# VectorE adds the residual rows before it divides the probabilities, in the steps that hold both

## The chip, the core and the metric

The kernel runs on one core of a Trainium2 chip. TensorE (PE) multiplies matrices into the accumulators (PSUM), VectorE (DVE), ScalarE (ACT) and GpSimd (POOL) do the elementwise work, SyncE (SP) issues the transfers. Each works through its own queue in order and waits for the others on counters (semaphores). The metric is the device time of one execution in microseconds; lower is better.

## What is computed

A decoder layer on x of 16 samples, 256 rows and 512 columns: windowed attention with 32 query heads and 8 key heads and a sink in each softmax, a convolution mixer on a second input, and a linear map by the mean of eight factors. Each is added to x behind a layer norm. The change lies in the attention:

```python
logits = jnp.einsum('bqhmd,bkhd->bhmqk', q, k) * SM_SCALE
...
e = jnp.exp(logits - m)
exp_sink = jnp.exp(s - m)
w = e / (jnp.sum(e, axis=-1, keepdims=True) + exp_sink)
out = jnp.einsum('bhmqk,bkhd->bqhmd', w, v).reshape(Bv, Tv, N_HEADS * HEAD_DIM)
return out @ out_w.T + out_b
...
x = x + _L0_attn_ref(_layernorm(x, axis=-1), ...)
```

## The kernel before

The attention goes over the 16 samples twice: the first sweep with one half of the heads, the second with the other (their weights are loaded and split between the two). A **window** is one sample in one sweep; there are 32. The first sweep writes x plus its half of the output projection to memory, the second adds its half to that and makes the layer norm for the mixer.

All engines run the same schedule, written out by hand. A loop body holds two windows, that is p = 0 to 7 and j = 0, 1; each (p, j) is a **step**, and a window has eight, numbered 2 * (p % 4) + j = 0 to 7. The bodies 2 to 6 and 10 to 14 are loops on the chip, the others are written out. The stages of a window are spread over three: while the projections ("units") of one window run, the scores of it and the output projection of the one before last are made.

TensorE does in a step: transposes of the divided probabilities (line 539, `pP`), a unit (lines 507, 514, `wP`) in steps 0, 1, 3, 5, 6 and 7, transposes of normalised rows in steps 2 and 4 (lines 462, 472), the scores (line 529, `sP`) in even steps, the value product (line 553, `vP`), and parts of the output projection (line 574, `oP`): 1, 2, 1, 2 and 1 of them in steps 1 to 5, and one in step 7. `oP` is a single accumulator. Parts 0 to 3 make tile t = 0 of the rows (128 of 256), begun in step 7 and ended in step 2; parts 4 to 7 make tile t = 1, steps 3 to 5. The first part of a tile waits until VectorE has added the tile before (`x1_ready`).

VectorE does in a step: `divide` (lines 856, 858, 864: the sum `den` of exponentials and sink, its reciprocal, four multiplications of `pr`) for the scores of the step before, `mask_transposed` (line 873, `pT`), in steps 3 and 7 `residual` (line 895: `x1` = `oP` + `xb`), then the rotation `turned` of a unit (line 823, `m1`) or the values (line 831), `mask_min` (lines 841, 847: mask the scores, take the row's minimum), `o_low` (line 882), and parts of layer norms (lines 778 to 790). `residual` of tile 0 stands in step 3, that of tile 1 in step 7.

ScalarE copies the transposed tile (line 655), adds the bias to a unit (line 633, `m2`), and takes the exponentials of the step's scores (lines 646, 649, `es`). GpSimd multiplies `m2` by its table (line 717), adds the two products (line 726), shifts the sinks (line 734), and in the first sweep, in step 2, adds the output bias to `xb` (line 759), two instructions for the two tiles; `residual` waits for both (`xb_ready`), in the second sweep for the transfer of `xb` instead.

The functions `residual_tile`, `divide`, `mask_transposed`, `residual` and VectorE's `body` are those that the change touches or moves.

Of the kernel before, what the change touches and what calls it, by code (L numbers as in the profile page):

```python
# [85 lines left out]
def attention_part(nc, x, wqkv, bqk, bv, wout, bout, sinks, rope, masks, ident, factors, ssm_pad, dcoef,  # L86
# [3 lines left out]
    with ExitStack() as ctx:  # L90
# [130 lines left out]
        def wait(eng, s, value):  # L221

            if isinstance(value, int) and value <= 0:
                return
            eng.wait_ge(s, value)
# [44 lines left out]
        def late(y, lag, p):  # L270

            if y.number is None:
                return y.sweep == 1
            return 2 * y.number + p // 4 - lag >= B
# [8 lines left out]
        def unit_of(p, j):  # L283
            return UNIT_AT.get(2 * (p % 4) + j)
# [8 lines left out]
        def residual_tile(y, p, j):  # L293

            return None if y.first else RESIDUAL_AT.get(2 * (p % 4) + j)
# [479 lines left out]
        def _(dve):  # L775
# [76 lines left out]
            def divide(y, u, j):  # L852
                h = 16 * y.m + 2 * u + j
                s = (2 * u + j) % 4
                dve.wait_ge(es_ready, h + 1)
                dve.tensor_tensor(den[:, s], ac[:, s], es[:, s], ALU.add).then_inc(den_ready, 1)  # L856
                dve.wait_ge(den_ready, h + 1)
                dve.reciprocal(rden[:, s], den[:, s]).then_inc(rden_ready, 1)
                dve.wait_ge(rden_ready, h + 1)
                for a in range(2):  # L860
                    for t in range(NT):
                        cols = slice(t * P, (t + 1) * P)
                        i = 2 * a + t
                        last = dve.tensor_scalar(pr[:, s, a, cols], pr[:, s, a, cols], rden[:, s, i:i + 1], None, ALU.mult)  # L864
                last.then_inc(pn_ready, 1)
# [19 lines left out]
            def residual(y, p, t):  # L885

                r = y.window(p) - 2
                old = late(y, 2, p)
                if old:
                    dve.wait_ge(xb_landed, 16 * r + 16)  # L890
                else:
                    dve.wait_ge(xb_ready, r + 1)
                dve.wait_ge(out_done, 8 * r + 4 * t + 4)
                wait(dve, x1_stored, 16 * r)
                dve.tensor_tensor(x1[:, t, :], oP[:], xb[:, t, :], ALU.add).then_inc(x1_ready, 1)  # L895
# [23 lines left out]
            def body(y):  # L919
                for p in range(8):  # L920
                    for j in range(2):
                        u, jj = (p - 3, 1) if j == 0 else (p - 2, 0)
                        if y.here(u, 0):
                            divide(y, u, jj)
                        if y.here(p, 3):
                            mask_transposed(y, p, j)
                        if residual_tile(y, p, j) is not None:
                            residual(y, p, residual_tile(y, p, j))
                        n = unit_of(p, j)
                        if n is not None and not y.drain:  # L930
                            if y.first and n == V_UNIT and p < 4:
                                dve.wait_ge(c_in, 16 * NCONST)
                            if n == V_UNIT:
                                v_evac(y, p)
                            else:
                                turned(y, p, rope_index(n))
                        if x_next(y, p, j):
                            x_low(y.window(p) + 1, (p // 4 + 1) % 2, p % 4 - 1)
                        if y.here(p, 2):
                            mask_min(y, p, j)  # L940
                        u, jj = (p - 4, 1) if j == 0 else (p - 3, 0)
                        if y.here(u, 0):
                            o_low(y, u, jj)
                        sl = 2 * (p % 4) + j
                        if sl in (4, 6) and x_after(y, p):
                            ln1_stats(y.window(p) + 2, (sl - 4) // 2)
                        if y.first and p == 0:
                            for t in range(NT):
                                if j == 0:
                                    ln1_stats(1, t)  # L950
                                else:
                                    ln1_end(1, t)
                        elif sl in (0, 1) and fresh(y, p):
                            ln1_end(y.window(p) + 1, sl)
                        if sl == 4 and late(y, 2, p):
                            ln2_stats(y.window(p) - 2, 0)
                        if sl == 0 and late(y, 3, p):
                            ln2_stats(y.window(p) - 3, 1)
                        if sl in (1, 2) and late(y, 3, p):
                            ln2_end(y.window(p) - 3, sl - 1)  # L960
                        for i, n in split_now(y, p, j):
                            split_low(i, n)
# [460 lines left out]
```

## Time and profile before

| | us |
|---|---|
| runs of the kernel | 2184.93, 2185.22, 2189.57 |
| their median | 2185.22 |
| the profiled execution | 2187.89 |
| its span, first to last instruction | 2185.7 |
| TensorE busy in it | 1988.6 |
| VectorE busy | 1610.8 |
| ScalarE busy | 935.4 |
| GpSimd busy | 771.3 |

The attention takes the stretch to about 1685 us, the rest is the mixer and the linear map, which the change doesn't touch. Times of the trace are counted from the span's start. An idle time in brackets stands behind the instruction that it precedes, with the work that ended it. In a row of merged instructions "x4" is their number, and the time is from the start of the first to the end of the last; instructions of one engine overlap a little, so that the next starts before the one ahead has ended. "issue" is time in which the engine waited for nothing that the profile shows.

### The profile page before, as it was taken

The page shows a single profiled execution, that of the slowest core. Times are in us where ns is not written, and L with a number is a line of the kernel's source. Part 1 is how long each engine was busy: PE and PEld are TensorE (multiplying, and loading weights), DVE is VectorE, ACT ScalarE, POOL GpSimd, SP SyncE. Part 2 cuts the span into 40 slices and gives each one's busy share as a digit, 9 for nine tenths or more (in the row PEclk, how much of TensorE's full clock was granted, in tenths as well). Part 3 has the DMA queues.
Part 4 walks back from the last instruction along what each step waited for, and adds up shares of the span by engine and source line. Part 5 has one row for each costly group of instructions (what it writes and reads, how often), then busy time and mean ns, then how long its engine had stood idle before and what let it go on. Part 6 is the DMA issues. An engine that isn't in the chain of part 4 may idle for free. (4 is left out here: it accounts for less than half of the span.)

```text
span 2185.7 us, 49034 instructions
## 1 busy us (share of the span) xinstructions
PE 1988.6 (91%) x15488; PEld 1619.9 (74%) x15488; DVE 1610.8 (74%) x5784; ACT 935.4 (43%) x3481; POOL 771.3 (35%) x879
## 2 busy tenths in 40 slices
PE   5799999999999989899999999999996899999699
PEld 4688877787877867778778777878774677677587
DVE  4777777776777766667767676767774699999787
ACT  3454545454545444444544454544542222222233
POOL 2244334333333333323322232223330454454354
PEclk8999999999999999999999999999998899999799
DMA  5147111111111121211111111111112633333364
GB/s 184 51 102 150 51 59 48 49 61 56 49 50 49 66 85 56 72 36 68 49 50 49 50 50 56 53 51 49 50 50 66 225 90 86 85 88 88 105 226 157
DMA packets 73966, 170.37 MB, mean 78 GB/s; under 512 B 6928, under 2 KB 15632, under 8 KB 73632
## 3 DMA queue, kind: packets, MB, share of 16 engines
q1 hardware_dynamic: 64160, 146.80, 20.4%
q0 software_dynamic: 3840, 8.39, 2.1%
q10 hardware_dynamic: 5760, 12.59, 1.5%
q8 instruction: 111, 1.82, 0.4%
q14 instruction: 95, 0.78, 0.1%
HBM read 109.03 MB, written 50.41 MB: 73 GB/s over the span
## 5 line engine op out<-in xcount | busy, mean ns | idle before, releaser
L646 ACT ACTIVATE pr<-pr,mx 128x128 f32<-128x128 f32 x1024 | 399.0, 391 | 441.5 <-DVE mx L847 441.5
L717 POOL TENSOR_TENSOR m<-m,rope_sb 128x512 f32<-128x512 f32 x160 | 206.6, 1291 | 563.2 <-ACT m L633 563.2
L514 PE MATMUL wP<-xTh,wh 128*128 128x256 f32 x1280 | 380.5, 297 | 5.8 <-DVE xTl L807 3.5
L514 PE MATMUL wP<-xTl,wh 128*128 128x256 f32 x1280 | 366.1, 286 | 0.0
L514 PE MATMUL wP<-xTh,wl 128*128 128x256 f32 x1280 | 364.7, 285 | 0.0
L1095 PE MATMUL y<-kv,tap 128*128 128x288 f32 x1280 | 330.1, 414 | 27.4 <-DVE res L1143 9.3
L1095 PEld LDWEIGHTS y<-kv,tap 128*128 128x128 f32 x1280 | 240.5, 192 | 116.9 <-issue 24.3
L856 DVE TENSOR_TENSOR den<-ac,es 128x4 f32<-128x4 f32 x256 | 63.1, 246 | 302.0 <-ACT es L649 270.5
L574 PE MATMUL oP<-woh,oTh 128*128 128x512 f32 x512 | 223.3, 436 | 55.0 <-DVE x L895 55.0
L514 PEld LDWEIGHTS wP<-xTh,wh 128*128 128x128 f32 x1280 | 248.7, 194 | 8.5 <-issue 3.1
L514 PEld LDWEIGHTS wP<-xTl,wh 128*128 128x128 f32 x1280 | 248.6, 194 | 0.0
L514 PEld LDWEIGHTS wP<-xTh,wl 128*128 128x128 f32 x1280 | 248.1, 194 | 0.0
L847 DVE CUSTOM_DVE_ANT_0 pr<-sP,mask_sb 128x128 f32<-128x128 f32 x1024 | 235.1, 284 | 0.5
L864 DVE TENSOR_SCALAR pr<-pr,rden 128x128 f32<-128x128 f32 x1024 | 224.6, 283 | 9.1
L553 PE MATMUL vP<-pT,vv 128*64 128x256 f32 (+1 forms) x2048 | 224.5, 340 | 0.9 <-DVE oTl L882 0.9
L633 ACT ACTIVATE m<-wP,bqk_sb 128x256 f32<-128x256 f32 x320 | 134.3, 471 | 210.7 <-PE wP L514 210.5
L734 POOL TENSOR_TENSOR sk<-mx,sink_sb 128x4 f32<-128x4 f32 x256 | 57.4, 224 | 458.8 <-DVE mx L847 458.8
L823 DVE SCALAR_TENSOR_TENSOR m<-wP,bqk_sb,rope_sb 128x256 f32<-128x256 f32 x320 | 139.4, 477 | 105.4 <-ACT m L633 105.0
L529 PE MATMUL sP<-kT,qT 32*128 32x128 f32 (+1 forms) x4096 | 209.7, 342 | 6.7 <-DVE mx L847 6.7
L1045 POOL TENSOR_TENSOR kv<-kk 128x1024 f32<-128x1024 f32 x64 | 144.1, 2251 | 182.8 <-PE y L1095 154.1
L574 PE MATMUL oP<-woh,oTl 128*128 128x512 f32 x512 | 203.8, 398 | 0.0
L574 PE MATMUL oP<-wol,oTh 128*128 128x512 f32 x512 | 203.7, 398 | 0.0
(108 smaller groups left out, 3781.8 us busy)
## 6 DMA issues: line engine op xcount, KB each, us to landing
tap<-padded_taps SPq DMA_DIRECT2D x64, 256.0 KB, 3.4
kk<-in_ctxt SPq DMA_DIRECT2D x64, 192.0 KB, 3.1
x_in<-in_x SPq DMA_DIRECT2D x16, 512.0 KB, 3.7
xt_split<-xTh SPq DMA_DIRECT2D x16, 512.0 KB, 3.1
xt_split<-xTl SPq DMA_DIRECT2D x16, 512.0 KB, 4.2
xb<-in_x SPq DMA_DIRECT2D x16, 512.0 KB, 4.5
fsum<-in_factors POOLq DMA_DIRECT2D x8, 1024.0 KB, 8.6
x_part_rows<-x SPq DMA_DIRECT2D x16, 512.0 KB, 3.1
```

The lines of the kernel that those rows point to most:

```text
L514: last = pe.matmul(wP[:, h * T:(h + 1) * T], w[:, n, c, h * P:(h + 1) * P], a[:, s, c, :], start=(c == 0 and i == 0), stop=(c == KD - 1 an ...
L529: last = pe.matmul(sP[:, r, t * P:P + 2 * t * P], qT[rr, p % 2, h, t * P:(t + 1) * P], kT[rr, kslot, h, 0:(t + 1) * P], start=(h == 0), st ...
L553: last = pe.matmul(vP[a * HD:(a + 1) * HD, k * P:T], vv[:, (u // 4) % 2, k, g * HD:(g + 1) * HD], pT[:, s, a, 2 * k * P:2 * P + k * P], st ...
L574: last = pe.matmul(oP[:], a[:, o, c, t * P:(t + 1) * P], w[:, c, :], start=(c == 0 and n == 0), stop=(c == NO - 1 and n == 2))
L633: last = act.activation(m2[:, s, 1 - half], wP[:, half * T:(half + 1) * T], ACT.Identity, bias=bqk_sb[:, y.sweep, i, half:half + 1])
L646: act.activation(pr[:, s, a, cols], pr[:, s, a, cols], ACT.Exp, bias=mx[:, s, i:i + 1], scale=-1.0, accum_out=ac[:, s, i:i + 1])
L717: pool.tensor_tensor(m2[:, s], m2[:, s], rope_sb[:, 1 if i == 0 else 0, 1:3], ALU.mult).then_inc(sin_ready, 1)
L823: last = dve.scalar_tensor_tensor(m1[:, s, half], wP[:, half * T:(half + 1) * T], bias[:, half:half + 1], tab[:, 0], ALU.add, ALU.mult)
L847: last = dve.tensor_tensor_reduce(pr[:, s, a, t * P:(t + 1) * P], sP[:, 2 * j + a, 2 * t * P:(2 * t + 1) * P], mask_sb[:, t * P:(t + 1) * ...
L864: last = dve.tensor_scalar(pr[:, s, a, cols], pr[:, s, a, cols], rden[:, s, i:i + 1], None, ALU.mult)
L1045: pool.tensor_tensor(kv[:, s, :, 0:4 * n].rearrange("p c (d n) -> p c d n", d=4), k0.unsqueeze(2).broadcast_to([P, KD, 4, n]), shifted, AL ...
L1095: last = pe.matmul(y[:, s, c, 0:NY], tap[:, s, d * P:(d + 1) * P], kv[:, s, c - d, :], start=(d == 0), stop=(d == c))
```

## The change

`residual` moves from behind `mask_transposed` to the front of VectorE's step. It happens in steps 3 and 7 of each window, 64 times in all. In 61 of them a division stands in the same step; at the very end of the attention three have none. The instructions, their waits and all other engines' programs are the same.

```diff
             def body(y):
                 for p in range(8):
                     for j in range(2):
+                        if residual_tile(y, p, j) is not None:
+                            residual(y, p, residual_tile(y, p, j))
                         u, jj = (p - 3, 1) if j == 0 else (p - 2, 0)
                         if y.here(u, 0):
                             divide(y, u, jj)
                         if y.here(p, 3):
                             mask_transposed(y, p, j)
-                        if residual_tile(y, p, j) is not None:
-                            residual(y, p, residual_tile(y, p, j))
```

VectorE in step 3 of the body 1, before; the first row is the last work of step 2, the last one the rotation of step 3:

```order
252 L882 TENSOR_TENSOR oTl<-vP,oTh 128x256
253 L856 TENSOR_TENSOR den<-ac,es 128x4
254 L858 RECIPROCAL rden<-den 128x4
255 L864 TENSOR_SCALAR pr<-pr,rden 128x128 x4
256 L873 TENSOR_TENSOR pT<-pP,mask_sb 128x2x256
257 L895 TENSOR_TENSOR x<-oP,xb 128x512
258 L823 SCALAR_TENSOR_TENSOR m<-wP,bqk_sb,rope_sb 128x256 x2
```

The same place now:

```order
252 L882 TENSOR_TENSOR oTl<-vP,oTh 128x256
253 L895 TENSOR_TENSOR x<-oP,xb 128x512
254 L856 TENSOR_TENSOR den<-ac,es 128x4
255 L858 RECIPROCAL rden<-den 128x4
256 L864 TENSOR_SCALAR pr<-pr,rden 128x128 x4
257 L873 TENSOR_TENSOR pT<-pP,mask_sb 128x2x256
258 L823 SCALAR_TENSOR_TENSOR m<-wP,bqk_sb,rope_sb 128x256 x2
```

The add of line 895 has passed seven instructions (den, the reciprocal, four multiplications and the masked transpose) and stands behind the work of step 2.

VectorE in step 7 of the same body, before; the first two rows are the layer norm at the end of step 6:

```order
316 L784 BN_AGGR mv<-stats 128x2 x2
317 L787 TENSOR_SCALAR veps<-mv 128x2
318 L856 TENSOR_TENSOR den<-ac,es 128x4
319 L858 RECIPROCAL rden<-den 128x4
320 L864 TENSOR_SCALAR pr<-pr,rden 128x128 x4
321 L873 TENSOR_TENSOR pT<-pP,mask_sb 128x2x256
322 L895 TENSOR_TENSOR x<-oP,xb 128x512
323 L823 SCALAR_TENSOR_TENSOR m<-wP,bqk_sb,rope_sb 128x256 x2
```

and now:

```order
316 L784 BN_AGGR mv<-stats 128x2 x2
317 L787 TENSOR_SCALAR veps<-mv 128x2
318 L895 TENSOR_TENSOR x<-oP,xb 128x512
319 L856 TENSOR_TENSOR den<-ac,es 128x4
320 L858 RECIPROCAL rden<-den 128x4
321 L864 TENSOR_SCALAR pr<-pr,rden 128x128 x4
322 L873 TENSOR_TENSOR pT<-pP,mask_sb 128x2x256
323 L823 SCALAR_TENSOR_TENSOR m<-wP,bqk_sb,rope_sb 128x256 x2
```

Here it has passed the same seven and stands behind the layer norm. The rotation follows line 873 directly in both steps.

## Rows read from the trace of the kernel before

**Rows 1.** The page, busy time of each engine, share of the span, instructions.
```profile
PE 1988.6 (91%) x15488; PEld 1619.9 (74%) x15488; DVE 1610.8 (74%) x5784; ACT 935.4 (43%) x3481; POOL 771.3 (35%) x879
```
**Rows 2.** TensorE's waits, 125:780, 780:960, 960:1640: us in total, times, longest.
```profile
PE oP L574 <- DVE x L895: 25.5, 26, 1.2
...
PE oP L574 <- DVE x L895: 14.4, 5, 4.8
...
PE oP L574 <- DVE x L895: 11.7, 14, 1.1
```
**Rows 3.** VectorE in order of time, step 3, first sweep: start, us, instruction.
```profile
430.91 0.98 DVE L856 TENSOR_TENSOR den<-ac,es 128x4 f32<-128x4 f32 x1 [1.48 <-ACT es L649]
...
432.14 0.87 DVE L864 TENSOR_SCALAR pr<-pr,rden 128x128 f32<-128x128 f32 x4
432.93 0.68 DVE L873 TENSOR_TENSOR pT<-pP,mask_sb 128x512 f32<-128x512 f32 x1
433.53 0.68 DVE L895 TENSOR_TENSOR x<-oP,xb 128x512 f32<-128x512 f32 x1
434.13 0.86 DVE L823 SCALAR_TENSOR_TENSOR m<-wP,bqk_sb,rope_sb 128x256 f32<-128x256 f32 x2
...
435.87 0.28 DVE L847 CUSTOM_DVE_ANT_0 pr<-sP,mask_sb 128x128 f32<-128x128 f32 x1
```
**Rows 4.** TensorE in order of time, the same step and the next.
```profile
434.26 0.50 PE L574 MATMUL oP<-woh,oTh 128*128 128x512 f32 x1 [1.09 <-DVE x L895]
...
436.74 1.59 PE L529 MATMUL sP<-kT,qT 32*128 32x128 f32 x32
```
**Rows 5.** GpSimd in order of time, the same step.
```profile
429.33 2.54 POOL L759 TENSOR_TENSOR xb<-xb,bo_sb 128x512 f32<-128x512 f32 x2
433.33 1.27 POOL L717 TENSOR_TENSOR m<-m,rope_sb 128x512 f32<-128x512 f32 x1 [1.46 <-ACT m L633]
```
**Rows 6.** VectorE and TensorE in order of time, step 7, first sweep.
```profile
455.83 0.16 DVE L856 TENSOR_TENSOR den<-ac,es 128x4 f32<-128x4 f32 x1 [0.27 <-ACT es L649]
...
458.36 0.50 PE L574 MATMUL oP<-woh,oTh 128*128 128x512 f32 x1 [0.80 <-DVE x L895]
```
**Rows 7.** VectorE in order of time, steps 5 and 0, first sweep.
```profile
446.44 0.88 DVE L823 SCALAR_TENSOR_TENSOR m<-wP,bqk_sb,rope_sb 128x256 f32<-128x256 f32 x2 [1.12 <-ACT m L633]
...
464.50 0.88 DVE L823 SCALAR_TENSOR_TENSOR m<-wP,bqk_sb,rope_sb 128x256 f32<-128x256 f32 x2 [0.54 <-ACT m L633]
```
**Rows 8.** GpSimd and VectorE in order of time, first body, 70 to 74 us.
```profile
70.83 1.27 POOL L717 TENSOR_TENSOR m<-m,rope_sb 128x512 f32<-128x512 f32 x1 [3.54 <-ACT m L633]
...
71.18 1.59 DVE L864 TENSOR_SCALAR pr<-pr,rden 128x128 f32<-128x128 f32 x4
```
**Rows 9.** GpSimd, VectorE and TensorE in order of time, 780:830.
```profile
784.15 1.31 POOL L717 TENSOR_TENSOR m<-m,rope_sb 128x512 f32<-128x512 f32 x1 [1.02 <-ACT m L633]
...
784.26 1.22 DVE L856 TENSOR_TENSOR den<-ac,es 128x4 f32<-128x4 f32 x1
...
787.85 0.55 PE L574 MATMUL oP<-woh,oTh 128*128 128x512 f32 x1 [4.24 <-DVE x L895]
...
801.15 0.88 DVE L823 SCALAR_TENSOR_TENSOR m<-wP,bqk_sb,rope_sb 128x256 f32<-128x256 f32 x2 [0.76 <-ACT m L633]
...
824.99 0.87 DVE L823 SCALAR_TENSOR_TENSOR m<-wP,bqk_sb,rope_sb 128x256 f32<-128x256 f32 x2 [1.15 <-ACT m L633]
```
**Rows 10.** Second sweep: order of time at steps 3 and 7, VectorE's waits of 960:1640.
```profile
1097.75 0.39 PE L574 MATMUL oP<-wol,oTh 128*128 128x512 f32 x1
...
1102.46 0.88 DVE L823 SCALAR_TENSOR_TENSOR m<-wP,bqk_sb,rope_sb 128x256 f32<-128x256 f32 x2 [2.16 <-ACT m L633]
...
1123.69 0.16 DVE L856 TENSOR_TENSOR den<-ac,es 128x4 f32<-128x4 f32 x1 [1.48 <-ACT es L649]
...
DVE m L823 <- ACT m L633: 59.1, 40, 2.9
```
**Rows 11.** One stretch: each engine's busy us, granted clock, DMA share, GB/s.
```profile
614.10:617.50 3.40, 3.40 (x19) 3.40 (x18) 1.81 (x7) 0.37 (x1) 0.00 (x0) 0.50 0.01 2
```

## The prediction, made before the changed kernel ran

> **What bounds the kernel now.** I read the shares of the page first, then TensorE's waits by stretch, then the order of time around single places of the residual add. TensorE is busy 1988.6 of 2185.7 us, VectorE 1610.8 [rows 1]: TensorE leads, and every stop of it is worth a look. The add (line 895) is waited for by the output projection (line 574) 25.5 us at 26 places in 125 to 780 us, 14.4 us at 5 in 780 to 960, 11.7 us at 14 in 960 to 1640 [rows 2]. These 51.6 us are the most the change could give. TensorE waits in the step in which the add stands: it has done its transposes, its unit and the value product, and needs the output accumulator empty.
>
> But TensorE is not alone on the path. VectorE masks the scores (lines 841, 847), ScalarE takes their exponentials, VectorE divides by their sum, multiplies the transposed tile with its mask (line 873) and only then reaches the next masking. TensorE's next scores wait for that masking. So a stop of TensorE that goes counts only until the next place at which VectorE is late. I go through one window (eight steps, numbered 0 to 7; adds in 3 and 7) for the first half of the heads, and one for the second.
>
> **Step 7, first half (13 places).** The projection waits 0.80 us [rows 6]; of the 25.5 us at 26 places the 13 of step 3 hold 14.5 (1.00 to 1.15 each, the shown one 1.09 [rows 4]), the 13 of step 7 the other 11.0 (0.80 to 0.90). The tile that the add empties was complete two steps before, so moved to the front it starts at once. It takes the next instruction 0.60 us later (432.93, 433.53, 434.13) [rows 3]. 0.27 us of it falls into VectorE's idle before the division [rows 6], so the division starts 0.33 later, and everything behind the old place 0.60 - 0.33 = 0.27 earlier. TensorE gains 0.80. At step 0 VectorE's rotation (line 823) is idle 0.54 for TensorE's unit [rows 7], so VectorE can follow by 0.27 + 0.54 = 0.81: the 0.80 passes on whole. **-11.0 us.**
>
> **Step 3, first half (13 places).** Here the add can't start at once. GpSimd adds the output bias to the same rows (line 759) until 429.33 + 2.54 = 431.87 [rows 5]; I count every time from that end, called E. Before, den (line 856) sat in front and lasted 0.98 us, until E + 0.02; the multiplications by the reciprocal (line 864) ran from E + 0.27, line 873 began at E + 1.06, the add at E + 1.66, the rotation at E + 2.26 [rows 3]. After: add at about E + 0.05, den E + 0.65, the four multiplications from E + 1.06 on, 0.20 apart, thus at 1.06, 1.26, 1.46 and 1.66. GpSimd's own multiplication (line 717) starts at 433.33 = E + 1.46, for 1.27 us [rows 5]: before, the four were over by then (431.87 + 1.14 = 433.01), now it falls among them. What such a meeting costs stands in the only place of the trace that has one: line 717 ran from 70.83 to 72.10, and the four multiplications beside it took 1.59 us [rows 8] where they take 0.87 [rows 3]; they ended 0.67 after GpSimd's end. So they don't run beside it. I take it that GpSimd comes in between two of the four: it then ends at about E + 2.75, two of the four follow, line 873 starts at E + 2.95 and the rotation at E + 3.55, that is 1.3 us later than before. If the four keep GpSimd out, the rotation starts at E + 2.45, 0.2 later.
>
> The Trainium skill, page "SBUF — State Buffer", section "Who interferes with whom", says that VectorE in a two-port mode and GpSimd share one port pair as an exclusive lock, that whoever issues first holds it for the whole instruction and the other fully blocks. By that rule GpSimd, issued ahead of the last multiplications, stops them, as I take it; the row at 71.18 agrees with the block, and no row shows who wins in the middle of four.
>
> For TensorE: its projection no longer waits (gain 1.09 at this place), but the masking ends at 435.87 + 0.28 = 436.15 and the scores began at 436.74 [rows 3, 4], a margin of 0.59, of which about 0.05 is the signal. With VectorE 1.3 later the scores start 1.3 - 0.54 = 0.76 later than before: the wait is not removed but moved, and grows. VectorE, 1.3 late, has 1.12 idle at step 5 [rows 7] plus TensorE's 0.76, so nothing more is added there. **13 x 0.77 = +10.0 us**; in the other branch the scores move by 0.2 - 0.54 = -0.33, thus 13 x -0.33 = -4.3.
>
> **780 to 960 (weights of the second half are split).** At three places (784, 812, 920 us) den comes behind a split of weights and is held by line 717: 784.26 for 1.22 us, until GpSimd's 784.15 + 1.31 = 785.46 [rows 9]. An add ahead of it runs in that hold and costs nothing, so VectorE gains the whole 0.60, three times 1.8. It can give back idle for TensorE behind two of them, 0.76 at 801 and 1.15 at 825 [rows 9]. Behind the third I count nothing. That is 3.7, with an ordinary step 7 place (0.8) 4.5. The wait of 4.24 [rows 9] does go, but TensorE then meets VectorE's transposed tile and its masking. Bounds: -1.8 and the stretch's -14.4 [rows 2]. **-4.5 us**, near the lower one, since the rows of VectorE's idle limit it.
>
> **Second half, 960 to 1640.** Step 7: den is idle 1.48 us [rows 10], more than the 0.60 of the add; the division doesn't move, the rotation comes up to 0.4 earlier, limited by ScalarE. The rotation is idle for TensorE's unit 59.1 us at 40 places of the stretch [rows 10], three in nearly every window (steps 0, 3 and 5), at step 0 never less than 0.40. So VectorE follows, and TensorE keeps its 0.8: **-11.7 us**, the whole row. Step 3: no wait of TensorE today, since VectorE is ahead. The last matmul for the tile ends at 1097.75 + 0.39 = 1098.14, so the add waits for it, and den behind it, until 1098.8; line 873 is through by 1100.7, and the rotation stands idle until 1102.46 anyway (2.16 idle) [rows 10]. Queued behind the waiting add are the division, the tile for the next value product and the rotation; the 1.8 us left hide them: 0, and about +1 a window if that cover went. The three last adds have no division behind them. The DMAs of the rows (SP queue) wait for the add of step 7 and get it earlier; GpSimd's queue is unchanged.
>
> **Sum**: -11.0 + 10.0 - 4.5 - 11.7 = -17.2 us. The profiled execution took 2187.89 us for a span of 2185.7; the median of the runs is 2185.22. I take the difference off the median: **2168 us**.
>
> **The clock** is granted 0.50, its lower level of 1.2 GHz, for 3.4 us behind a loop end (614.1 to 617.5) [rows 11]; it fell so behind six of the eight loop ends between equal iterations. 3.4 us at half speed cost 1.7. Before each, TensorE had been idle for the add and then some 2.9 us for the loop's return. With the first idle gone, falls may vanish or move: between -10 and +3 us, counted as none in the sum.
>
> **The rivals.**
> - GpSimd doesn't get between the four multiplications. For it: they follow each other 0.20 apart while each lasts 0.28, without a gap. Against it: the row at 71.18, and that GpSimd asks 0.2 us before the last one. Sum: -11.0 - 4.3 - 4.5 - 11.7 = -31.5, **2154 us**.
> - The gains of TensorE don't pass the next masking: VectorE's idle at step 0 is used up, and each step 7 gives only VectorE's 0.27, in the second half 0.40. 13 x (0.77 - 0.27) - 14 x 0.40 - 4.5 = -3.6, **2182 us**. Against it stand the idles of 0.54 and more [rows 7, 10].
> - Slower: the cycle of VectorE and ScalarE sets the pace of the first half, and the hold by GpSimd at step 3 stays in it. Place: the rotation of step 5. It decides once the idle there (1.12 [rows 7]) can't take the 1.3. Each window then costs 1.3 - 0.27 = 1.03; 13 x 1.03 = 13.4, less VectorE's own gains elsewhere (1.8 from the three holds, 14 x 0.40 = 5.6 in the second half): +6.0, **2191 us**.
> - That the change doesn't do what it says I exclude: 61 of 64 adds have a division behind them, and the three at the end cost nothing.
>
> **How the numbers follow.** Forecast 0.6, two-port meeting avoided 0.25, gains not passed on 0.08, slower 0.05, 0.02 for what I don't see. Of this kernel 0.2%, 4.4 us, is about what a measurement can tell from no change. Faster by more than that: 0.85; within: 0.09; slower: 0.06. The forecast's own range is 2158 to 2175 (clock, and 0.5 to 1.0 instead of 0.77 at step 3). For 8 in 10 it must reach into the second branch: 2149 to 2177.
>
> **What would show it.** The waits of line 574 for line 895 nearly vanish in all three stretches. At step 3 of the first half line 864 takes about 2 us for its four beside line 717, and TensorE waits instead at the scores (line 529) for line 847, about 0.8 us more each, some 10 us in all; if line 864 stays at 0.87 and line 717 lengthens by some 0.4, the second branch is true. At step 7 of both halves nothing replaces the wait. At step 3 of the second half VectorE waits for line 574 before the add, and the idle of the rotation falls from 2.16 to about 1.8 less whatever TensorE gained. A window of the first half lasts as long as before, one of the second 0.8 less. The forecast is wrong if line 864 isn't held, if the clock falls at other places more than twice as often, or if a wait for line 873 or 864 appears at TensorE's transposes.

## The result and the profile after

| | before | after |
|---|---|---|
| median of the runs, us | 2185.07 | 2170.89 |
| lowest and highest of 6 runs | 2184.27, 2189.57 | 2167.07, 2176.24 |
| profiled execution | 2187.89 | 2171.32 |
| its span | 2185.7 | 2169.2 |

The ratio of after to before is 0.9935, with a 95% interval of 0.9919 to 0.9951: 14.2 us faster by the medians, 16.5 by the two spans. The prediction said 2168 us, 17.2 faster.

Busy times hardly moved [rows 1]. The page of after:

```profile
PE 1991.8 (92%) x15488; PEld 1615.7 (74%) x15488; DVE 1615.5 (74%) x5784; ACT 935.1 (43%) x3481; POOL 771.7 (36%) x879
```

So the gain is idle time of TensorE. Its waits of after in 125:780, 780:960 and 960:1640 (total, times, longest), the answer to [rows 2]:

```profile
PE pP L539 <- DVE pT L873: 16.5, 17, 1.2
PE sP L529 <- DVE mx L847: 9.0, 18, 0.6
...
PE pP L539 <- DVE pT L873: 10.4, 9, 2.6
PE sP L529 <- DVE mx L847: 5.8, 7, 1.3
PE oP L574 <- DVE x L895: 5.0, 3, 1.9
...
PE wP L472 <- DVE xn L790: 19.2, 14, 1.5
```

The waits of the output projection for the add, 51.6 us before, are gone but for 5.0 in the middle stretch. In the first sweep 25.5 us for the add have turned into 16.5 for line 873 (4.1 us at 3 places before) and 9.0 for line 847 (1.4 at 4).

**Step 3, first sweep.** All engines of after in order of time, the answer to [rows 3 to 5]; the add waits for GpSimd's bias, whose end E is here 432.07:

```profile
432.31 0.69 DVE L895 TENSOR_TENSOR x<-oP,xb 128x512 f32<-128x512 f32 x1 [2.69 <-POOL xb L759]
432.92 0.15 DVE L856 TENSOR_TENSOR den<-ac,es 128x4 f32<-128x4 f32 x1
433.27 0.50 PE L574 MATMUL oP<-woh,oTh 128*128 128x512 f32 x1
433.31 1.96 DVE L864 TENSOR_SCALAR pr<-pr,rden 128x128 f32<-128x128 f32 x4
433.49 1.30 POOL L717 TENSOR_TENSOR m<-m,rope_sb 128x512 f32<-128x512 f32 x1 [1.43 <-ACT m L633]
...
435.19 0.68 DVE L873 TENSOR_TENSOR pT<-pP,mask_sb 128x512 f32<-128x512 f32 x1
435.80 0.86 DVE L823 SCALAR_TENSOR_TENSOR m<-wP,bqk_sb,rope_sb 128x256 f32<-128x256 f32 x2
436.02 0.63 PE L539 MATMUL pP<-id_sb,pr 128*128 128x128 f32 x4 [1.08 <-DVE pT L873]
...
437.88 0.50 PE L529 MATMUL sP<-kT,qT 32*128 32x128 f32 x8 [0.51 <-DVE mx L847]
```

The projection (433.27) no longer waits. But line 717 came in 0.18 us after the first multiplication had begun, and the four took 1.96 us instead of 0.87. TensorE pays 1.08 at the transposes of the next step and 0.51 at its scores. The four take 1.91 to 2.00 us at all 13 places of step 3. One of the four bears it, 1.32 to 1.41 us instead of 0.28: the second at ten places, where line 717 starts 0.15 to 0.22 us after the first, and the fourth at three, where it starts 0.47 or 0.48 after. TensorE pays as here at the ten and 0.74 and 0.59 at the three.

Six more such meetings with line 717 stand in the trace of after and none of them in that of before (the one near 71 us [rows 8] is in both): in step 0 behind three of the four loop ends of the first sweep (413.64, 514.51, 613.85), and at 795.02, 826.92 and 933.11.

```profile
413.64 1.96 DVE L864 TENSOR_SCALAR pr<-pr,rden 128x128 f32<-128x128 f32 x4
```

**Step 7 and step 0, first sweep**, the answer to [rows 6, 7]: the add starts at once, the projection does not wait, and at step 0 the rotation has no idle left.

```profile
456.71 0.69 DVE L895 TENSOR_TENSOR x<-oP,xb 128x512 f32<-128x512 f32 x1
457.31 0.15 DVE L856 TENSOR_TENSOR den<-ac,es 128x4 f32<-128x4 f32 x1
458.64 0.50 PE L574 MATMUL oP<-woh,oTh 128*128 128x512 f32 x1
464.77 0.88 DVE L823 SCALAR_TENSOR_TENSOR m<-wP,bqk_sb,rope_sb 128x256 f32<-128x256 f32 x2
```

**780 to 960 and the second sweep**, the answer to [rows 9, 10]. The division behind the first add is held 0.64 us, not 1.22. At step 3 the add waits 1.38 for the last matmul, and the rotation's idle fell from 2.16 to 1.80. At step 7 the add stands in VectorE's idle, of which 0.88 of 1.48 is left.

```profile
781.54 0.64 DVE L856 TENSOR_TENSOR den<-ac,es 128x4 f32<-128x4 f32 x1
...
1089.06 0.69 DVE L895 TENSOR_TENSOR x<-oP,xb 128x512 f32<-128x512 f32 x1 [1.38 <-PE oP L574]
...
1093.35 0.88 DVE L823 SCALAR_TENSOR_TENSOR m<-wP,bqk_sb,rope_sb 128x256 f32<-128x256 f32 x2 [1.80 <-ACT m L633]
...
1114.57 0.16 DVE L856 TENSOR_TENSOR den<-ac,es 128x4 f32<-128x4 f32 x1 [0.88 <-ACT es L649]
```

**The length of a window** is the measure that the waits don't give. I take it from the start of one add of step 3 to the next, between two windows of one loop body; such windows agree within 0.1. Before (the other end is 433.53 [rows 3]) and after (432.31 above):

```profile
482.10 0.68 DVE L895 TENSOR_TENSOR x<-oP,xb 128x512 f32<-128x512 f32 x1
```
```profile
480.93 0.69 DVE L895 TENSOR_TENSOR x<-oP,xb 128x512 f32<-128x512 f32 x1 [2.65 <-POOL xb L759]
```

That is 48.57 and 48.62: a window of the first sweep is as long as before. One of the second fell from 48.95 to 48.09. Windows with a loop end between their adds are longer: 51.37, 52.32, 53.39 and 53.22 before, 50.73, 50.56, 52.15 and 50.76 after, in the first sweep. For sums over stages the add is a poor mark, since the change moves it by different amounts in the two sweeps and not at all in the last window, where no division stands behind it. I take the start of TensorE's scores in step 4 instead, before and after at the end of the first sweep and at the last window:

```profile
737.95 1.59 PE L529 MATMUL sP<-kT,qT 32*128 32x128 f32 x32
1611.18 1.59 PE L529 MATMUL sP<-kT,qT 32*128 32x128 f32 x32
```
```profile
735.56 1.59 PE L529 MATMUL sP<-kT,qT 32*128 32x128 f32 x32 [0.58 <-DVE mx L847]
1595.91 1.59 PE L529 MATMUL sP<-kT,qT 32*128 32x128 f32 x32
```

By these, after is 4.3 us shorter from 139 to 738 us (twelve windows), 3.9 from there to 957, 9.0 from 957 to 1611 and 1.3 behind. Up to 139 us it is 1.9 longer, 1.1 of it before the first scores. Together that is the 16.5 of the spans.

### The profile page after: what moved, and what is told of

It is laid out like the page before. It is cut to its first block and busy times, and to the rows that moved or that the text cites. A ratio compares the mean times of both kernels' runs of the same rounds, so it can differ in the third digit from the quotient of the medians.

```text
span 2169.2 us, 49034 instructions
## 1 busy us (share of the span) xinstructions
PE 1991.8 (92%) x15488; PEld 1615.7 (74%) x15488; DVE 1615.5 (74%) x5784; ACT 935.1 (43%) x3481; POOL 771.7 (36%) x879
## 5 line engine op out<-in xcount | busy, mean ns | idle before, releaser
L864 DVE TENSOR_SCALAR pr<-pr,rden 128x128 f32<-128x128 f32 x1024 | 245.4, 303 | 9.1
L856 DVE TENSOR_TENSOR den<-ac,es 128x4 f32<-128x4 f32 x256 | 46.9, 183 | 244.8 <-ACT es L649 227.1
L539 PE MATMUL pP<-id_sb,pr 128*128 128x128 f32 x1024 | 159.2, 278 | 59.2 <-DVE pT L873 40.6
```

The lines of the kernel that those rows point to most:

```text
L539: last = pe.transpose(pP[:, (2 * a + t) * P:(2 * a + t + 1) * P], pr[:, (2 * p + 2 + j) % 4, a, t * P:(t + 1) * P], id_sb[:])
```

## The experiments

The lengths of plain windows (first sweep, second sweep) and the four windows with a loop end in the first sweep, all from the profiled execution, and the median of 4 to 12 runs:

| kernel | first | second | with a loop end, first sweep | us |
|---|---|---|---|---|
| before | 48.57 | 48.95 | 51.37, 52.32, 53.39, 53.22 | 2185 |
| after | 48.63 | 48.09 | 50.73, 50.56, 52.15, 50.76 | 2171 |
| s7_only | 47.70 | 48.07 | 49.66, 49.48, 49.60, 49.48 | 2160 |
| s3_only | 49.50 | 48.94 | 53.97, 56.66, 54.23, 53.01 | 2205 |
| hold_pool | 47.55 | 48.07 | 49.56, 49.49, 51.03, 49.53 | 2152 |
| split_xb | 46.55 | 48.07 | 48.85, 48.82, 48.55, 48.61 | 2142 |
| split_late | 47.77 | 48.95 | 50.58, 50.57, 52.49, 50.56 | 2177 |
| s7_and_s3b | 47.70 | 48.07 | 49.58, 50.85, 49.82, 49.81 | 2161 |
| s3_hold | 48.43 | 48.94 | 51.24, 51.26, 52.23, 51.27 | 2185 |
| s3_first | 49.50 | 48.94 | 54.06, 54.39, 53.30, 56.01 | 2207 |
| s7_store_late | 47.70 | 48.06 | 49.60, 49.65, 49.64, 49.47 | 2155 |
| before_quiet | 48.57 | 48.95 | 49.03, 48.89, 48.91, 53.94 | 2178 |
| split_quiet | 46.55 | 48.07 | 48.39, 48.27, 48.72, 50.23 | 2126 |
| s7_store_mid | 47.70 | 48.06 | 50.54, 50.47, 51.41, 51.32 | 2162 |

### One step alone: s7_only and s3_only

```diff
+                        if residual_tile(y, p, j) is not None and (residual_tile(y, p, j) == 1):
+                            residual(y, p, residual_tile(y, p, j))
                         u, jj = (p - 3, 1) if j == 0 else (p - 2, 0)
...
-                        if residual_tile(y, p, j) is not None:
+                        if residual_tile(y, p, j) is not None and not (residual_tile(y, p, j) == 1):
                             residual(y, p, residual_tile(y, p, j))
```

s7_only (s3_only has 0 for 1):

> The add goes first in step 7 alone; in step 3 it stands behind line 873 as in the kernel before. Theory A (in the changed kernel the add at step 3 of the first sweep lets GpSimd's line 717 come in between the four multiplications of line 864, which costs TensorE 0.8 us a window, 10 us in all, and step 7 gives the gain): about 2160 us, ten below the changed kernel's 2171; TensorE waits 1.1 us for line 895 at each step 3 of the first sweep and not for line 873 or 847 there; the four of line 864 take 0.87. Theory B (the meeting is hidden, and step 3 costs nothing or gives a part of the gain): 2171 us or more. Theory C (steps 3 and 7 only give together): 2185.

> The add goes first in step 3 alone; in step 7 it stands behind line 873 as before. Theory A: slower than before, 13 windows by 0.8 us less some 2 us at the place where line 717 holds den anyway: 2192 us (2188 to 2196). Theory B: 2185 or a few below. The sum of what this and the step 7 kernel move against the kernel before should be what the whole change moved, -14 us, if the two places don't influence each other.

s7_only took 2160.47 us (ratio 0.9884, 0.9869 to 0.9900), s3_only 2204.63 (1.0086, 1.0069 to 1.0102). A window of the first sweep got 0.87 shorter by the one and 0.93 longer by the other, which add up to the +0.06 of after. So in plain windows the two steps are independent: -0.87 x 13 = -11.3 us for step 7, where the prediction has 11.0, and +0.93 x 13 = +12.1 for step 3, where it has 10.0. The second sweep is shorter by 0.88 with step 7 alone and unchanged with step 3 alone. The medians don't add up (-24 and +20 against -14); the spans of the profiled executions, from which the windows are read, do so nearly (-35.5 and +17.0 against -16.5). The profiled execution of s7_only, 2152.34 us, is the fastest of its five runs. s7_only came out as expected, s3_only 8 us above its range: what its windows don't explain lies mostly at the loop ends, below.

### Without the meeting: hold_pool and s3_hold

```diff
                 pool.wait_ge(bent_ready, (QM + 1) * v + i + 1)
+                if i == 2 and not y.first and not late(y, 2, p):
+                    pool.wait_ge(pn_ready, 16 * y.m + 2 * (p - 2) + 1)
```

GpSimd waits before line 717 until VectorE's four multiplications are done. hold_pool is this edit on the whole change, s3_hold on s3_only.

> The changed kernel, but GpSimd waits in step 3 of the first sweep for the division (pn_ready) before its line 717; nothing else differs, VectorE's order and the start of the add least. Theory A (the loss is GpSimd holding line 864): the four of line 864 take 0.87 instead of 1.97 beside line 717, the rotation comes 1.1 us earlier, 13 times 0.9 us go: about 2159 us. Rival (the loss is that the add waits for GpSimd's rows xb and pushes the division back): 2171, since that wait stays.

hold_pool took 2152.48 us (0.9852, 0.9835 to 0.9870), 18 us less than the change alone. In order of time:

```profile
425.06 0.87 DVE L866 TENSOR_SCALAR pr<-pr,rden 128x128 f32<-128x128 f32 x4
...
426.08 1.28 POOL L719 TENSOR_TENSOR m<-m,rope_sb 128x512 f32<-128x512 f32 x1 [2.27 <-DVE pr L866]
```

(Two lines were added, so 866 is 864 and 719 is 717.) The four are back at 0.87 us and the window at 47.55, 1.08 us below after; 13 of them are 14 us, a little more than expected. The meeting is the cause of step 3's price. By the spans hold_pool is 21.2 us shorter than after. The rest over 14 is hardly at the loop ends of the first sweep (0.3 us): 1.6 us are a fall of the clock that after has near 238 us and hold_pool hasn't, and some 5 lie behind 738 us.

> The add is first in step 3 only, as in s3_only, and GpSimd holds its multiplication of line 717 in step 3 of the first sweep until VectorE has divided. s3_only took 2204.6 us, 20 more than before, where its plain windows explain 13 x 0.93 = 12. Theory A (all of it hangs on GpSimd's multiplication among the four of VectorE; the 8 us over 12 are what follows at loop ends): windows of the first sweep fall from 49.50 to about 48.4 (s7_only 47.70 to hold_pool 47.55 says 0.15 under the order of before) and the total to 2180, within 5. Rival B (something else of the move costs, the late division itself): windows stay above 48.8 and the total above 2190.

s3_hold took 2184.63 us (1.0004, 0.9993 to 1.0016), at the upper end of what was expected, its windows 48.43, as expected. Without the meeting the add in front at step 3 is worth 0.14 a window: one way and the other it is the meeting that counts.

### Where the 20 us of s3_only are: s3_first, and s7_and_s3b

The same edit as above, with `and not late(y, 2, p)` for s3_first (first sweep alone) and `== 1 or late(y, 2, p)` for s7_and_s3b.

> The add is first in step 3 of the first sweep alone; step 7, and step 3 of the second sweep, are as before. Theory A: the same as s3_only in every plain window, 49.50 in the first sweep and 48.93 in the second, so 2184 + 12 = 2196 from the windows; the 8 us that s3_only had above this were two or three long returns of the loop in the first sweep (windows with a loop end of 53.97 and 56.66 where before had 51.37 and 52.32), with falls of the clock. If these are chance, they change here and the total is 2194 to 2205; if they belong to the late VectorE, they stand here again and the total is 2204 within 3. Rival B (the second sweep has a share in the 20 us): total below 2194 with the same windows in the first sweep.

> The add is first in step 7 everywhere, and in step 3 of the second sweep alone; in step 3 of the first sweep it stands where it stood before. Theory A (the move at step 3 of the second sweep is worth nothing, since TensorE is never waited for there and the rotation has over a microsecond of idle): the same as s7_only, 2160 us within 4, windows of the first sweep 47.70 and of the second 48.07. Rival B (the held-back division does cost there): windows of the second sweep longer by 0.1 to 1 us, 2162 to 2175. What the whole change lacks against this, 2171 - 2160 = 11, is then the price of step 3 in the first sweep alone: 13 x 0.93 = 12.

s3_first took 2206.86 us (1.0101, 1.0087 to 1.0115), as slow as s3_only: the second sweep has no share in it. s7_and_s3b took 2160.58 (0.9894, 0.9880 to 0.9909), the same as s7_only. Both say that step 3 of the second sweep costs nothing.

In both kernels with the bare step 3 the windows with a loop end exceed their own plain ones by 19.8 us in all, before by 16.0, and s3_hold by 12.3. One plain window (233 to 284 us, with a fall of the clock at 238) is 1.6 longer too. 12.1 + 3.8 + 1.6 = 17.5, and the scores at 738 us come 17.0 later. The excess came in both kernels with the bare meeting and went in the one without it, so it hangs on the meeting as well. TensorE's granted clock over 125:780, s3_first and s3_hold:

```profile
125.00:780.00 655.00, 612.03 (x5415) 0.98 0.22 65
```
```profile
125.00:780.00 655.00, 624.49 (x5607) 1.00 0.23 69
```

With the meeting TensorE stands more, and more of the time is at 1.2 GHz rather than 2.4 (before 0.99). Which of the two brings the other at the loop ends is not shown. A few us between the medians are left over, in which the runs of before also spread.

### The bias split: split_xb and split_late

```diff
-                            for t in range(NT):
-                                last = pool.tensor_tensor(xb[:, t, :], xb[:, t, :], bo_sb[:], ALU.add)
-                            last.then_inc(xb_ready, 1)
+                            pool.tensor_tensor(xb[:, 0, :], xb[:, 0, :], bo_sb[:], ALU.add).then_inc(xb_ready, 1)
+                        if p % 4 == 2 and j == 0 and not y.first and not late(y, 2, p):
+                            pool.tensor_tensor(xb[:, 1, :], xb[:, 1, :], bo_sb[:], ALU.add).then_inc(xb_ready, 1)
...
-                    dve.wait_ge(xb_ready, r + 1)
+                    dve.wait_ge(xb_ready, 2 * r + t + 1)
```

split_xb has this on the changed order, split_late on that of before.

> The changed kernel, but GpSimd adds the bias to the rows of tile 0 in step 2 and to those of tile 1 in step 4, and each add waits for its own tile only. The add of step 3 can then start about 1.3 us earlier, inside the idle before den, and the division ends before line 717 starts. Theory A: neither the add's wait nor the meeting is left, line 864 takes 0.87, TensorE keeps the 1.1 us of step 3 too: 2143 to 2148 us. Rival (TensorE's gain at step 3 does not pass the next masking, since VectorE with ScalarE sets the pace there): 2157 to 2160, no better than holding GpSimd back.

split_xb took 2141.62 us (0.9800, 0.9783 to 0.9818), a little below theory A's range. At step 3 the add now starts 1.27 us earlier against GpSimd's other work (1.68 us behind the start of its line 734 instead of 2.95), the four multiplications are through when line 717 asks, and a window takes 46.55 us:

```profile
416.91 0.69 DVE L895 TENSOR_TENSOR x<-oP,xb 128x512 f32<-128x512 f32 x1 [1.42 <-POOL xb L758]
417.92 0.87 DVE L864 TENSOR_SCALAR pr<-pr,rden 128x128 f32<-128x128 f32 x4
419.33 1.30 POOL L717 TENSOR_TENSOR m<-m,rope_sb 128x512 f32<-128x512 f32 x1 [2.66 <-ACT m L633]
```

> The order of before (add behind the masked transpose), but GpSimd adds the bias to tile 0 in step 2 and to tile 1 in step 4, and the add waits for its own tile alone. It tells how much of split_xb's 43 us is the order and how much the split by itself. In the window before, the division of step 3 was held by GpSimd's two bias adds for 0.98 us where it lasts 0.16; with one of them gone from step 2, GpSimd is done 1.27 us earlier. Theory A (order and split each bring their own part): VectorE's rotation comes about 0.75 us earlier than before, TensorE keeps waiting 1.1 us for the add at step 3, windows of the first sweep 47.8 to 47.9 us instead of 48.57 (13 x 0.7 = 9 us), those of the second 48.94 as before: about 2175 us, so the order is worth some 33 us once the bias add is split. Theory B (the split does all): windows of the first sweep near the 46.55 of split_xb and a total below 2160. Theory C (TensorE waits for the add in place of everything else): windows as before, 2184.

split_late took 2176.62 us (0.9965, 0.9951 to 0.9979), windows 47.77: as expected. The order that is worth 14 us by itself is worth 35 once the bias is split: the meeting at step 3 is gone, and TensorE's wait for the add with it.

### VectorE's return at a loop end: s7_store_late, before_quiet, split_quiet, s7_store_mid

s7_only's windows with a loop end shrank by 1.7 to 3.8 us, where a plain one lost 0.87. The idle of VectorE in front of the first division of a body shows it. Before, the last instruction of a body, ScalarE's sums, and the division:

```profile
307.95 0.42 DVE L882 TENSOR_TENSOR oTl<-vP,oTh 128x256 fp32r<-128x256 f32 x1
309.62 0.19 ACT L649 ACTIVATE es<-sk 128x4 f32<-128x4 f32 x1
312.53 0.92 DVE L856 TENSOR_TENSOR den<-ac,es 128x4 f32<-128x4 f32 x1 [4.17 <-issue]
```

The sums were ready at 309.81; the return to the loop's start cost 4.17 us, 2.7 of them past that. s7_only and after at the same kind of place:

```profile
406.35 0.16 DVE L856 TENSOR_TENSOR den<-ac,es 128x4 f32<-128x4 f32 x1 [2.29 <-ACT es L649]
```
```profile
413.23 0.16 DVE L856 TENSOR_TENSOR den<-ac,es 128x4 f32<-128x4 f32 x1 [2.31 <-ACT es L649]
```

At the four loop ends of the first sweep it is 3.96 to 4.5 us in every kernel so far with the add of step 7 behind, and 2.2 to 2.6 in every one with it in front. Not all of it reaches the window: in s7_only the earlier division meets line 717, and the four of line 864 in step 0 take 1.89 us at all four places. The transfers differ: SyncE issues the store of the rows and the load of the next ones (512 KB each) after that add. The share of the DMA engines in tenths, in slices of 0.35 us, of before in 302:316 and of s7_only in 396:410:

```profile
DMA  0000000000000069999948972000000000000000
```
```profile
DMA  0000000000000099999689920000000000000000
```

Before, they run from about 307 to 310.7, and VectorE leaves at 308.37 in their midst. In s7_only they run from 401 to 404.4, and it leaves at 404.06, when they are nearly over. The edits hold SyncE back at loop ends:

```diff
                     sp.wait_ge(x1_ready, 2 * r + 2)
+                    if y.number is None and a == 1 and y.sweep == 0:
+                        sp.wait_ge(ot_lo, 16 * m + 9)
```

This is s7_store_late, on s7_only. s7_store_mid waits for `pt_masked` (16 * m + 10) instead. before_quiet (on before) and split_quiet (on split_xb, both sweeps) wait for `den_ready` (16 * m + 12), the first division of the next body.

> As s7_only, but at the four loop ends of the first sweep SyncE issues the store of the finished rows (and the load of the next, 512 KB each) only once VectorE is through step 7, some 4 us later, so that the 4 us of transfers lie over VectorE's return to the loop's start. It tests why s7_only gained 24 us where its windows explain 13 x 0.87 + 14 x 0.87 = 23.5 only if nothing changes at loop ends, yet windows with a loop end shrank by more: VectorE was idle 3.96 to 4.19 us from its last instruction to the division of step 0 before, and 2.25 to 2.42 in s7_only. Theory A (the store and load delay the return; put forward by the earlier add, they are over when it comes): VectorE's idle at these four places is 3.7 us or more again, windows with a loop end rise from 49.5 to 50.4 or more, the total by 4 to 10 us, to 2164 to 2170. Rival B (the return is short for another reason, such as what stands in front of the branch): idle stays at 2.2 to 2.6, total 2160.

It took 2154.86 us (0.9856, 0.9835 to 0.9876), the idle 2.27 to 2.45: a miss for A. But the hold was too long for the test. The DMA share in slices of 0.175 us, 402:409, and a queue of that stretch (packets, MB, share):

```profile
DMA  0000000020006999999999358987997430010000
...
q14 instruction: 2, 0.02, 0.8%
```

VectorE left at 403.23, and the transfers began only at 404.1. Ahead of them, at 403.57, stands a lone packet of 8 KB, of the queue that loads instructions.

> The order of before. At the four loop ends of the first sweep SyncE holds the same store and load until VectorE has begun the division of step 0, that is until its return is over. Theory A (transfers delay the return): VectorE's idle there falls from 4.0 to 2.2 to 2.6, windows with a loop end from 51.4 to 53.4 to about 50.5, the total by 4 to 10 us: 2174 to 2180. Rival B (something else): idle stays near 4.0, total 2184.

before_quiet took 2178.35 us (0.9965, 0.9949 to 0.9981), as theory A has it. The idle is 2.42 to 2.52, and three of four windows with a loop end are only 0.3 to 0.5 longer than a plain one. In the fourth TensorE itself returned late:

```profile
604.41 1.11 PE L541 MATMUL pP<-id_sb,pr 128*128 128x128 f32 x4 [3.64 <-issue]
604.60:607.90 3.30, 3.30 (x18) 0.55 0.87 288
```

(the second row is that stretch: the clock was mostly at its lower level).

> As s7_only, with the store and load of the four loop ends of the first sweep held until VectorE's masked transpose of step 7, which ends 2.3 us before VectorE's last instruction, just as the add of before did. In s7_store_late the hold was too long: VectorE left at 403.23, the transfers started at 404.4 and the return took 2.45 us, no more than without a hold. In before they had run from 307.2 when VectorE left at 308.37. Theory A, narrowed (what counts is that the transfers are in flight at the moment VectorE leaves): idle 3.7 us or more again at the four places, windows with a loop end 50.4 to 53 instead of 49.5, total 4 to 12 us above s7_only, 2160 to 2168. Rival B (the time of the transfers is without effect, only the place of the add ahead of the branch): idle 2.2 to 2.6 and 2153 to 2160.

s7_store_mid took 2161.94 us (0.9894, 0.9876 to 0.9912). VectorE leaves at 404.73, the transfers run from 403.3 to 406.8 (the share in 396:410 below), and the idle is 4.07 to 4.43 again; windows with a loop end are 0.9 to 1.8 longer than s7_only's:

```profile
408.80 0.35 DVE L858 TENSOR_TENSOR den<-ac,es 128x4 f32<-128x4 f32 x1 [4.07 <-issue]
```
```profile
DMA  0000000000000000000009999995995000000000
```

So it is the time of the transfers, not the place of the add, that sets the return: VectorE's order is that of s7_only.

The packets tell where the time goes. In each return one packet of 8 KB of the instruction queue q14 starts between VectorE's leaving and the division. Before, VectorE leaves at 308.37; the queues of 308.40:310.50, then of 310.50:310.60, and of s7_only, where it leaves at 404.06, in 404.40:404.50 (the first stretch has no packet of q14):

```profile
q1 hardware_dynamic: 297, 0.56, 91.3%
```
```profile
q14 instruction: 1, 0.01, 19.3%
```
```profile
q14 instruction: 1, 0.01, 30.8%
```

That is 2.2 us after leaving with the transfers under way (q1) and 0.35 without, and the division follows 1.95 and 1.94 us behind the packet's start. So it is at all 112 loop ends of the fourteen kernels: the packet starts 0.3 to 0.7 us after VectorE has left in the returns of up to 2.6 us, 1.5 to 2.6 us after it in the longer ones, and the division always 1.9 to 2.2 us later.

The four windows of s7_store_mid are 5.5 us longer in sum and the span 4.5. The median lies only 1.5 above s7_only's, where 4 to 12 were expected; s7_store_late, with windows like those of s7_only, came out 5.6 below it, so medians of kernels with the same windows differ by that much.

> split_xb with the same hold at the loop ends of both sweeps. In the second sweep every kernel had an idle of VectorE of 3.4 to 4.2 us there, with four transfers of 512 KB behind each other over it. Theory A: they fall to 2.2 to 2.6 in the second sweep too, four windows get shorter by 1 to 3 us (51.0, 51.3, 53.1, 54.1 now), so 2131 to 2138 against 2141.6, unless the later loads are then waited for, which would show as VectorE's wait before the add of step 3 and a time above 2142. Rival B: 2141 within 4.

split_quiet took 2125.81 us (0.9719, 0.9700 to 0.9739), the fastest of all and 5 us below theory A's range. In the second sweep the idle is 2.20 to 2.24, where every other kernel has 3.4 to 4.2, and the windows with a loop end are 49.21 to 49.42 instead of split_xb's 51.0 to 54.1:

```profile
1089.82 0.16 DVE L858 TENSOR_TENSOR den<-ac,es 128x4 f32<-128x4 f32 x1 [2.24 <-ACT es L651]
```

TensorE's own idle at the first transposes behind the branch is shorter there too, 0.91 to 1.14 us, in split_xb 2.73 to 3.27.

## Why the prediction was right, point by point

- **Sum.** 2168 predicted, 2170.89 measured; -17.2 predicted, -16.5 by the spans. The mechanism at steps 3 and 7 came as forecast. Of the sizes, step 3 cost 2.1 us more and the two later stretches gave 0.6 and about 2 less, while the loop ends, counted as none, gave 6.3, of which a fall of the clock near 238 us took 1.6 back. That these errors nearly cancel is luck; that the sum is a gain of this order is not.
- **Step 7, first sweep**: -11.0 predicted; -0.87 x 13 = -11.3 by s7_only. The rotation of step 0 has used up its idle, as said.
- **Step 3, first sweep**: +10.0 predicted, +0.93 x 13 = +12.1 measured. GpSimd did get between the four, as the row at 70.83 suggested [rows 8]. The size was a little off (the 0.76 of the prediction's own subtraction, carried as 0.77, against 0.93) because the add began at E + 0.24, not E + 0.05, so that line 717 came in after the first multiplication, not the second, and the four took 1.96. The rotation began at E + 3.73 instead of E + 3.55. The rule cited from the Trainium skill, page "SBUF — State Buffer", section "Who interferes with whom", held in what it says of the block: one of the four took 1.32 to 1.41 us instead of 0.28. The run adds that a row of VectorE's multiplications doesn't keep GpSimd out from one to the next, since GpSimd got in 0.18 us after the first had begun.
- **Where TensorE pays at step 3**: predicted only at the scores, 0.76 each; measured 1.08 at the transposes for line 873 and 0.51 at the scores. What I had wrong there: I followed VectorE to its masking and left out that TensorE's transposes of step 4 need line 873 of step 3. By my own numbers it ended at E + 3.63 = 435.50, while the projection, without its wait, ended at about 434.84: the wait was there to be read. I even named a wait for line 873 as a sign that the forecast is wrong. It was none: it is the same delay, met earlier. What decides is the window's length, which is 48.57 and 48.63, "as long as before".
- **780 to 960**: -4.5 predicted, -3.9 measured (738 to 957, TensorE's scores). The held division shrank from 1.22 to 0.64, and of the wait for line 895 5.0 us stay at 3 places. Three new meetings of line 717 with the four multiplications (795, 827 and 933 us) were not foreseen.
- **Second sweep**: -11.7 predicted, -9.0 measured up to the last scores, -9.6 up to the last output projection. The plain windows gave 0.86 each, where 0.84 was forecast. But its four windows with a loop end shrank by 1.0 in sum instead of 3.4. Step 3 costs nothing there, as s7_and_s3b shows.
- **Loop ends**: counted as none, with -10 to +3 for the clock. In the first sweep they gave -6.3 us (9.7 us over plain windows instead of 16.0). The range held it, the reason did not: I looked at TensorE's idle for the add before the branch. What changed first is VectorE's return, 4.0 to 2.4 us, since the transfers that the add lets go are nearly over when it leaves. The 6.3 are of two kinds. In windows in which the clock doesn't fall, a loop end costs 2.8 us over a plain window before (one window; s3_hold and split_late have 2.8 in three each) and 1.9 to 2.1 after, some 3 us for four. That isn't the whole 1.6 of the return; the new meetings with line 717 fit this, for before_quiet, with as short a return and without them, has 0.3 to 0.5. And the clock fell in three of the four windows before and in one after, which is the rest. Why those falls went is not shown. The prediction said of these transfers only that they "get it earlier". The clock still falls, at other places, such as inside a body of after, where one window took 50.22:

```profile
238.00:241.00 3.00, 3.00 (x34) 0.50 0.00 0
```

- **The first sweep in sum**: 12 windows of +0.06 are 0.7, loop ends -6.3, the fall at 238 +1.6, together -4.0 of the 4.3 measured.
- **The rivals.** The two-port meeting avoided (2154) did not come about by itself, but hold_pool brought it about: 2152. Gains not passed on, and slower, fell with s7_only. That slower is a real case the runs of s3_only show: where only the add of step 3 is moved, the hold isn't paid for by step 7.

## What to carry to other kernels

An instruction moved ahead of others shifts all of them against every other engine: before the move, list what runs beside the new times, above all GpSimd's work beside VectorE's multiplications, and follow each delayed tile to all its readers, not only to the last. Price a step in a loop by the length of a plain window, and the loop ends apart, since a total mixes both with the clock; for sums take a mark that the change doesn't move. Where a transfer of some hundred KB isn't urgent, let it start once the engines are through the branch of a loop: with a split bias and such a hold this kernel came from 2185 to 2126 us, of which the change of order alone gave 14.

## What the runs showed of the hardware that was not expected

- **VectorE's return to a loop's start takes longer while transfers run.** It took 2.2 to 2.6 us when the DMA engines were idle or nearly done as it left, and 3.4 to 4.5 when it left in the midst of the transfers; those that began 0.9 us after it had left did no harm (2.45). The Trainium skill, page "Runtime: NRT & Kernel Launch", section "Instruction fetch mechanics", says that a taken branch whose target is outside what the engine has loaded forces a DMA fetch before it can go on. The trace agrees: in each of the 112 returns a packet of 8 KB of an instruction queue starts 1.9 to 2.2 us ahead of the division, and what the transfers delay is that start, from 0.3 to 0.7 us to 1.5 to 2.6. That VectorE waits for this packet is read from these times alone.
- **One GpSimd operation of 1.30 us stretches four VectorE multiplications of 128x128 from 0.87 to 1.96 us**, by 1.09, though it asked after they had begun. One of the four bears it, 1.32 to 1.41 instead of 0.28. The meeting appears wherever the times fall together, in after at 13 places of step 3 and 6 others.
- Open: why single returns of TensorE last 3.6 to 4.2 us (604 us in before_quiet, 420 in s3_only), and what sets at which loop end the clock falls. No run was aimed at either.
